# An early-fusion image and text block on one core: projection and FFN as three float32r products each, with low parts by GpSimd, and other steps moved

## What is computed

```
red = grid.mean(axis=(3, 5))                      # mean of a window
q, kv = ln(red) @ la_wq, ln(win) @ la_wkv
local_out = red + softmax(q k) v @ la_proj_w + la_proj_b   # over the 9 cells
patch_out = local_out @ mod_w + mod_b
cls_out = cls + attention(cls, local_out) @ ga_proj_w + ga_proj_b
```

## Time and profile before

| what | value |
|---|---|
| median of 3 runs | 766.26 us (765.4 to 767.36) |
| the profiled execution's own time | 761.81 us |
| its span, first to last instruction | 760.1 us |
| PE busy | 690.5 us, 91% of the span |
| DVE busy | 535.0 us, 70% |
| POOL busy | 422.3 us, 56% |
| ACT busy | 394.8 us, 52% |
| mean granted TensorE clock | 0.960 of 2.4 GHz |
| read and written in HBM | 33.69 MB and 11.40 MB |

### The profile page before, as it was taken

The page is one execution under the profiler, slowest core; times in us unless marked ns, Lnnn a source line. Parts: engine busy times, 40 slices in busy tenths (PEclk is TensorE's granted clock), DMA queues, the critical chain, the costliest instruction groups (busy, mean ns, idle before and its releaser), DMA issues.

```text
span 760.1 us, 23650 instructions
## 1 busy us (share of the span) xinstructions
PE 690.5 (91%) x9239; PEld 550.9 (72%) x9239; DVE 535.0 (70%) x1208; ACT 394.8 (52%) x969; POOL 422.3 (56%) x450
## 2 busy tenths in 40 slices
PE   5998969989987288999999999999999999999873
PEld 3987847778874166778778877878887887887651
DVE  2468585686877457678878878878878878866632
ACT  4563432634542145666666666666566566565431
POOL 3667371483643755475575575575675675663221
PEclk9999988999998589999999999999999999999997
DMA  9950470532220022222332332232232232122100
GB/s 221 237 143 1 119 222 1 145 77 47 62 60 22 19 58 69 76 64 67 79 74 74 77 80 72 77 78 74 74 77 76 73 77 78 39 61 57 35 20 25
DMA packets 69524, 58.69 MB, mean 77 GB/s; under 512 B 30607, under 2 KB 68646, under 8 KB 69286
## 3 DMA queue, kind: packets, MB, share of 16 engines
q1 hardware_dynamic: 69414, 57.18, 29.3%
HBM read 33.69 MB, written 11.40 MB: 59 GB/s over the span
## 4 chain that ended last, share of the span: by engine, by line
PE 75%; DVE 12%; DMA 4%; issue 3%; ACT 3%; POOL 2%; SPq 1%; POOLq 0%; DVEq 0%; ACTq 0%
PE p_a L1309 13%; PE p_c L1309 13%; PE p_s L1369 6%; PE p_conv L764 6%; PE p_o L1381 6%; PE p_kv L764 6%; PE p_n L1389 4%; PE p_c L1429 4%; PE p_s L1351 4%; PE p_a L1335 3%; PE p_s L1365 2%; PE p_mm L764 2%; PE p_c L1410 2%; DMA h<-h_tokens 2%; PE p_n L1395 2%
## 5 line engine op out<-in xcount | busy, mean ns | idle before, releaser
L1244 DVE TENSOR_REDUCE mx<-p_s 87x16 bf16<-87x1392 f32 x64 | 101.6, 1587 | 23.5 <-PE p_s L1351 23.4
L1104 POOL TENSOR_TENSOR t<-t,ss_rs 116x512 f32<-116x512 f32 x48 | 50.9, 1060 | 118.3 <-ACT ss_rs L1151 117.1
L1175 ACT ACTIVATE prT<-p_s 87x1392 f32<-87x1392 f32 x64 | 85.1, 1329 | 58.9 <-PE p_s L1369 57.4
L426 POOL TENSOR_TENSOR xs_lo<-xcols,xs_hi 120x585 fp32r<-120x585 f32 (+1 forms) x45 | 60.5, 1351 | 56.9 <-ACT xs_hi L489 56.9
L1100 POOL TENSOR_TENSOR t<-t 116x512 f32<-116x512 f32 x48 | 61.1, 1274 | 22.9 <-DVE t L1235 22.9
L1369 PE MATMUL p_s<-qr,kr 32*87 32x87 f32 x2048 | 68.4, 256 | 0.0
L1107 POOL TENSOR_TENSOR t<-t,tabs 116x512 f32<-116x512 f32 x48 | 63.0, 1312 | 3.8
L1309 PE MATMUL p_c<-w_f,yT 128*116 128x296 f32 x192 | 58.2, 426 | 2.0 <-ACT yT L1194 0.9
L1369 PEld LDWEIGHTS p_s<-qr,kr 32*87 32x87 f32 x2048 | 60.0, 153 | 0.0
L1365 PE MATMUL p_s<-mxT,pick_row 32*87 32x87 bf16 x1024 | 55.6, 207 | 1.4 <-ACT mxT L1169 1.4
L1381 PE MATMUL p_o<-prT,vp 87*32 87x87 f32 x2048 | 54.7, 246 | 0.0
(11 more groups left out here) (248 smaller groups left out, 1892.5 us busy)
## 6 DMA issues: line engine op xcount, KB each, us to landing
xcols<-in_x_cols SPq DMA_DIRECT2D x12, 822.7 KB, 12.1
h<-h_tokens SPq DMA_DIRECT2D x16, 348.0 KB
out<-out_sb SPq DMA_DIRECT2D x48, 116.0 KB
h_tokens<-in_txt SPq DMA_DIRECT2D x4, 1232.0 KB, 11.7
x<-in_txt_cols SPq DMA_DIRECT2D x32, 154.0 KB, 2.7
qr<-qkT SPq DMA_DIRECT2D x64, 58.0 KB, 2.0
kr<-qkT SPq DMA_DIRECT2D x64, 58.0 KB, 2.0
vp<-vt SPq DMA_DIRECT2D x32, 87.0 KB
```

Of the source, the lines that this page charges most:

```text
L426: nc.gpsimd.tensor_tensor(xs.lo[:, n % XS_SLOTS, :, 0:M].bitcast(F32R), raw, xs.hi[:, n % XS_SLOTS, :, 0:M], ALU.subtract).then_inc(S['xs_ ...
L1104: link(nc.gpsimd.tensor_tensor(t4, t4, ss_rs[:, b].unsqueeze(2).broadcast_to([TP, 2 * HEADS, HD]), ALU.mult))
L1175: nc.scalar.activation(prT[:, k % 2], p_s[0:SEQ, :, 0:QUADS * SEQ], ACT.Exp, scale=HD ** -0.5).then_inc(S['s_exp'], 1)
L1244: nc.vector.reduce_max(mx[:, k % 2, :, 0:QUADS], p_s[0:SEQ, :, 0:QUADS * SP].rearrange("p j (a k) -> p j a k", k=SP)[:, :, :, 0:SEQ], AX_X ...
```

## The change

The projection and the FFN become split products. Their weights get a high part (ScalarE) and a low part (GpSimd) once, in group 0. Their inputs are evicted twice by ScalarE, as they are and rounded to float32r, and GpSimd subtracts one from the other (`oB_lo`, `yT_lo`); TensorE waits for the low part. Beside it: the loads x.1 and x.2 get earlier due times; the centring goes to other cells of windows 2 and 3; the clears are made in two parts, one behind `xc` of group 1, one behind `add.0` of group 0; in the last window the sum over the cells is made by TensorE; the gate's exponential takes the negated maximum as its bias; the last group uses banks A and C in turn; hb of group 0 and the first exponential wait for aggT, not agg. All five tables of the groups are new, with a period of 276 and a start of 2070.

```diff
@@ order tables @@
-                score.2.498 s_max.0.517 att.0.538 sum.0.593 sum.1.638 lo.0.695 lo_var.0.700 patch.0.730 gv.0.752
+                score.2.498 s_max.0.517 att.0.538 sum.0.620 sum.1.638 lo.0.695 lo_var.0.700 patch.0.730 gv.0.752
-WINDOW_SP = table("""x.0.-398 x.1.-64 x.2.-30 rows.0.736 cls.0.970""")
+WINDOW_SP = table("""x.0.-398 x.1.-317 x.2.-245 rows.0.736 cls.0.970""")
...
+                oT.1.510 mT.3.525 oT.2.536 exp.3.542 oB.0.575 oB.1.633 oT.3.647 oB.2.662 oB.3.734 yT.0.762
+                yT.1.778 rstd_c.0.875 ffn.0.881 ffn.1.904 yT.2.916 ffn.2.944 gate.0.1004 twT.0.1086""")
...
+                oN.3.674 oB.3.715 proj.0.722 proj.1.739 yT.0.756 yT.1.771 proj.2.838 ffn.0.869 ffn.1.890
+                yT.2.911 ffn.2.932 twT.0.1072 lora.0.1092 lora.1.1232""")
...
+GROUP_POOL = table("""xc.0.-264 xlo.0.-86 add.0.33 scale.0.63 shift.0.110 add.1.153 scale.1.166 shift.1.177 add.2.220 scale.2.249
+                shift.2.260 hb.0.571 oB_lo.0.599 hb.1.676 oB_lo.1.683 oB_lo.2.688 oB_lo.3.768 hb.2.786
+                yT_lo.0.856 yT_lo.1.880 yT_lo.2.925 base.0.931 above.0.969 base.1.1036 base.2.1070""")
+GROUP_SP = table("""cols.0.-400 rows.0.-276 place.0.210 values.0.258 place.1.291 values.1.438 store.0.1111 store.1.1115 store.2.1253""")
-GROUP_PERIOD, GROUP_START = 288, 2100
+GROUP_PERIOD, GROUP_START = 276, 2070
@@ patch_tokens @@
-        CENTRE_PE, CENTRE_DVE = (3, 5, 6), (3, 4, 6)
-        CLASS_PE, CLASS_DVE = ((1, 2), (1, 4), (1, 6)), ((0, 6), (1, 0), (1, 4), (1, 6))
+        CENTRE_PE, CENTRE_DVE = ((2, 6), (2, 7), (3, 6)), ((2, 5), (2, 6), (3, 5))
+        CLASS_PE, CLASS_DVE = ((1, 2), (1, 4), (1, 6)), ((0, 6), (1, 0), (1, 4), (1, 5))
...
-                    if s == STEPS - 1 and k == 0:
-                        pool.wait_ge(S['conv'], CELLS * STEPS)
-                        pool.wait_ge(S['kv_mm'], CELLS * STEPS)
-                        pool.wait_ge(S['stat'], CELLS * STEPS)
-                        pool.wait_ge(S['red'], (CELLS - 1) * STEPS)
-                        clear()
...
-                if name == 'sum':
+                if name == 'sum' and s < STEPS - 1:
...
-                    pe_.wait_ge(S['agg'], s + 1)
-                    transpose(p_T, agg[0:M], M).then_inc(S['aggT'], 1)
+                    if s < STEPS - 1:
+                        pe_.wait_ge(S['agg'], s + 1)
+                        transpose(p_T, agg[0:M], M).then_inc(S['aggT'], 1)
+                    else:
+                        pe_.wait_ge(S['vw'], PIECES * (s + 1))
+                        for c in range(CC):
+                            part = slice(C + P * c, C + P * (c + 1))
+                            mm_ = mm(p_T[:, c, 0:M], [kv[0:M, ring(s, j), i, part] for j in range(PIECES) for i in range(LOAD_CELLS)]
+                                     + [bias_kv[0:1, part]], [ident[0:M, 0:M]] * CELLS + [consts.ones[0:1, 0:M]])
+                        mm_.then_inc(S['aggT'], 1)
@@ attention_ffn @@
+        LAST_BANK = {'tile': 'ACA', 'gate': 'A', 'lora': 'CA'}
+
+        def bank(what, g, k):
+
+            return LAST_BANK[what][k] if g == GROUPS - 1 else 'C'
...
-            def clear():
-
+            def clear_strips():
+
+                pool.wait_ge(W['conv'], CONVS)
                 for part in (qr, kr, mx):
                     ready(nc.gpsimd.memset(part[:], 0.0))
+
+            def clear_values():
+
+                pool.wait_ge(W['kv_mm'], CONVS)
+                pool.wait_ge(W['stat'], CONVS)
+                pool.wait_ge(W['red'], (CELLS - 1) * STEPS)
                 ready(nc.gpsimd.memset(vp[:, :, :, HD:], 1.0))
                 ready(nc.gpsimd.memset(twT[TILES * LR:TILES * LR + 1], 1.0))
...
+                    if g == 1:
+                        clear_strips()
...
+                    if g == 0 and k == 0:
+                        clear_values()
...
+                if name == 'oB_lo':
+                    pool.wait_ge(S['oB_out'], GB * g + k + 1)
+                    if k == 0:
+                        wait(pool, S['proj'], 3 * (g - 1))
+                    part = (slice(None), half, slice(None), slice(SEQ * k, SEQ * (k + 1)))
+                    nc.gpsimd.tensor_tensor(onT.lo[part].bitcast(F32R), on_raw[:, k % 2], onT.hi[part],
+                                            ALU.subtract).then_inc(S['oB_low'], 1)
+                if name == 'yT_lo':
+                    pool.wait_ge(S['yT_out'], 3 * g + k + 1)
+                    wait(pool, S['ffn'], 3 * g + k - 1)
+                    nc.gpsimd.tensor_tensor(yT.lo[:, b].bitcast(F32R), y_raw[:, b], yT.hi[:, b], ALU.subtract).then_inc(S['yT_low'], 1)
...
+                    if g == 0 and k == 1:
+                        for n, (w, raw) in enumerate(((wp, w_p), (wf, w_f))):
+                            pool.wait_ge(S['w2_high'], n + 1)
+                            nc.gpsimd.tensor_tensor(w.lo[:].bitcast(F32R), raw[:], w.hi[:], ALU.subtract).then_inc(S['w2_low'], 1)
...
+                    if g == 0:
+                        act.wait_ge(W['agg'], STEPS - 1)
+                        act.wait_ge(W['kv_mm'], CONVS)
+                        act.wait_ge(consts.w_in, 16 * consts.LOADS)
+                        act.wait_ge(consts.S['w_sub'], 3 * CC)
+                        nc.scalar.copy(wp.hi[:].bitcast(F32R), w_p[:]).then_inc(S['w2_high'], 1)
+                        nc.scalar.copy(wf.hi[:].bitcast(F32R), w_f[:]).then_inc(S['w2_high'], 1)
...
-                    nc.scalar.copy(onT[:, half, :, SEQ * k:SEQ * (k + 1)],
+                    wait(act, S['oB_low'], n4 - 2)
+                    nc.scalar.copy(on_raw[:, k % 2], p_n[:, 0:CC * SP].rearrange("p (c q) -> p c q", c=CC)[:, :, 0:SEQ])
+                    nc.scalar.copy(onT.hi[:, half, :, SEQ * k:SEQ * (k + 1)].bitcast(F32R),
...
-                    nc.scalar.copy(yT[:, b], p_c[:, 0:CC * TP].rearrange("p (c n) -> p c n", c=CC)).then_inc(S['yT_out'], 1)
+                    wait(act, S['yT_low'], n3 - 2)
+                    nc.scalar.copy(y_raw[:, b], product('tile', g, k)[:, 0:CC * TP].rearrange("p (c n) -> p c n", c=CC))
+                    nc.scalar.copy(yT.hi[:, b].bitcast(F32R), product('tile', g, k)[:, 0:CC * TP].rearrange("p (c n) -> p c n", c=CC)).then_inc(S['yT_out'], 1)
...
-                    nc.scalar.activation(g_e[:], g_e[:], ACT.Exp).then_inc(S['g_exp'], 1)
+                    act.wait_ge(S['ffn_out'], 3 * g + 3)
+                    wait(act, S['tw_ok'], g)
+                    for tile in range(TILES):
+                        last = nc.scalar.activation(g_e[:, tile], f[:, half, tile, C + LR:FFN_N], ACT.Exp, bias=g_max[:, tile:tile + 1])
+                    last.then_inc(S['g_exp'], 1)
...
-                    link(nc.vector.reduce_max(g_max[:], lg, AX_X))
-                    nc.vector.tensor_tensor(g_e[:], lg, g_max[:].unsqueeze(2).broadcast_to([TP, TILES, EXPERTS]),
-                                            ALU.subtract).then_inc(S['g_m'], 1)
+                    wait(dve, S['g_exp'], g)
+                    nc.vector.reduce_max(g_max[:], lg, AX_X, negate=True).then_inc(S['g_m'], 1)
...
-                    mm(p_c[0:TP, 0:C], [onT[:, half, c, TP * k:TP * (k + 1)] for c in range(CC)],
-                       [w_p[:, c] for c in range(CC)]).then_inc(S['proj'], 1)
+                        pe.wait_ge(S['w2_low'], 2)
+                    pe.wait_ge(S['oB_low'], GB * g + min(k + 1, GB - 1) + 1)
+                    mm_split(product('tile', g, k)[0:TP, 0:C], onT.chunks(lambda x_, c: x_[:, half, c, TP * k:TP * (k + 1)]),
+                             wp.chunks(lambda x_, c: x_[:, c])).then_inc(S['proj'], 1)
...
-                    pe.wait_ge(S['yT_out'], n3)
-                    mm(p_c[0:TP, 0:FFN_N], [yT[:, b, c] for c in range(CC)], [w_f[:, c] for c in range(CC)]
-                       ).then_inc(S['ffn'], 1)
+                    pe.wait_ge(S['yT_low'], n3)
+                    mm_split(product('tile', g, k)[0:TP, 0:FFN_N], yT.chunks(lambda x_, c: x_[:, b, c]), wf.chunks(lambda x_, c: x_[:, c])
+                             ).then_inc(S['ffn'], 1)
```

85 lines of the change are left out of this document (39 added, 46 removed).

## The result

| | before | changed |
|---|---|---|
| median | 765.83 us (4 runs, 764.44 to 767.36) | 811.97 us (4 runs, 802.94 to 818.05) |
| ratio | | 1.0563, 95% interval 1.0474 to 1.0651 |
| profiled execution, span | 761.8, 760.1 us | 818.05, 816.3 us |
| PE busy | 91% | 87% |
| ACT, POOL, DVE busy | 52%, 56%, 70% | 53%, 59%, 66% |

The forecast was 735.5 us.

What follows compares the result with a forecast made beforehand. TensorE's own time was taken to bound the steady stage. Products -17.3, weights +1, windows -9, transition -4, banks -3, last chain +1.5 sum to -30.8: 761.8 to 731.0, plus 4.5 for the median, 735.5 us; range 727 to 747.

Steps and rivals of the forecast that it cites:

- The other cover of group 0 (later token loads): Transition: group 0's later token loads have 7 us from due time to first use; no cost was added.
- All five rivals: Queues 0.20, windows give nothing back 0.17, yT low parts never hidden 0.04, products no faster 0.02, all better 0.07.
- the slower one: Steady groups: TensorE idles before each ffn for copy and subtraction, period 30.7, 784 us; chance 0.04.
- The stage table: Groups 3 to 15: TensorE has work in 344.49 of 344.5 us, so only TensorE's own time counts there.
- Products: Projection and FFN tiles: three products save 0.36 us a tile, 1.08 us a group, -17.3 us in all.
- What pays for it: Low parts and second evictions: nothing in the steady stage; weights' low parts in group 0 cost +1 us.
- The rival of the queues: Steady groups: more GpSimd work makes waits more frequent, period 28.2, +9 us, 744.5 us; chance 0.20.
- Windows: Windows 2 and 3: earlier loads and moved centring remove waits and low clock; -9 us, between -3 and -12.
- Transition: Between windows and steady groups: clears moved out of window 4's weightings; -4 us, between -8 and +2.
- The sum: Window 4: 40 records on TensorE, 5.3 us or twice that at low clock, replace 5.8 us of VectorE's sum.
- End: Tail: two banks in turn give -3 us, the last chain's copies and low parts cost +1.5 us.
- the latency's 1.5 us: Tail: a copy and a low part at oB.3 and yT.2 in the last chain, +1.5 us after overlap.

Runs made afterwards that it cites:

- e2: Changed kernel with SyncE's token load due at -310 instead of -276, ahead of the transposed values' transfers; 755.3 us, ratio 0.985.
- e11: Kernel before with only the token load due at -475 instead of -500, behind the transposed values' transfers; 794.81 us, ratio 1.036.
- e18: Changed kernel, all due times kept, with each group's token load issued as two transfers (rows 0 to 111, 112 to 115); 754.95 us, ratio 0.988.
- e3: Changed kernel with float32 projection and FFN, no low parts, single evictions, new order tables kept; 823.92 us.
- e16: e2 with the last window's sum put back on VectorE; 745.26 us.
- e12: e4 with the last window's sum put back on VectorE; 741.38 us, ratio 0.965.
- e9: e2 with the float32 products of before; 758.18 us.
- e10: Whole change on the group order of before, low parts put in behind their evictions; 756.28 us.
- e4: Changed kernel with float32 products and the old group tables, period and start; 748.06 us, ratio 0.976.
- e15: e12 with the FFN product alone in three products, projection still float32; 748.66 us.
- e7: e4 with the windows' input loads back at their old due times on SyncE; 757.84 us.
- e8: e4 with the centring of the weights back at its old cells of window 2; 760.96 us.
- e17: e16 with float32 products from single evictions in the last group only; 744.88 us.

## Why the prediction was wrong

**The step that failed** is the one that cost the later token loads at nothing: "The other cover of group 0 (later token loads) has 7 us from its due time to its first use." Three things were wrong in it. It asked for group 0 alone, where the load comes in every group. It took a distance of due times (7.4 us) for time at hand, and neither looked up how long the load takes to land (8.7 and 8.9 us where its reader waited in the kernel before, 10.1 us at its new place) nor what it stands behind on SyncE; what a moved load stands behind was asked for the windows' loads and not for this one. And it named no one who waits: behind the statistics on VectorE stands `max.1`, and behind that TensorE. e2, e11 and e18 show it, from three sides: issue it earlier, issue it later in the kernel before, make it land sooner. All five rivals and their chances missed it; the slower one (low parts of yT never hidden) had a period of 30.7 us by another mechanism, which e3 refutes.

**The stage table** was read rightly, that the steady stage is TensorE's alone. But a full TensorE says only that nothing was late then, not by how much nothing was late. The load had mostly 9.7 to 10.6 us from issue to first use, and may have needed some 8.8: a margin of one or two microseconds, where the change took away 2.9 by the due times and made the landing longer by more than one.

**Products**, -1.08 us a group: mis-sized. Measured -0.68, -0.03 and +0.86 by the order, and -0.52 between e16 and e12, two kernels without waits for tokens. The tiles themselves gave 0.95 and 0.80 us. The pace of a pair was right (0.28 and 0.24 us), the tile was taken as six of them: first and last pair take 0.05 to 0.09 us more each where a 32-row product follows, and an FFN tile in the changed order takes 0.98 us, not 0.82. The float32 tile depends on its neighbours too: in e9 an FFN tile takes 1.12 to 1.16 us, in e12 0.99 to 1.09.

**What pays for it**, nothing in the steady stage: not so. The low parts are as long as estimated, and TensorE doesn't wait for them by name. But with three products it idles more (0.43 us a group in e10 against e4, 0.41 in e15 against e12, 0.14 in e2 against e9), and products beside them take longer. The rival of the queues had the size (e2's period of 28.43 us is near its 28.2) and in part the kind; its waits for onT_lo and yT_lo are not the ones seen, which are for kr, for h and for ScalarE's eviction.

**Windows**, -9 us: measured -15.1 at group 0's start, past the far end of -12. Both parts are right in kind. The loads were mis-sized: undoing them costs 6.0 us (e7), where they had a share of 2.5, because they take waits out of windows 3 and 4 too. The centring gave 7.3 us (e8) for a net 6.5.

**Transition**, -4 us: measured +4.0. The wait of 12.1 us is 5.6 us in the changed kernel, as forecast. The larger part of the miss is the same late load, which groups 2 and 3 wait for already: with the load issued earlier (e2) the transition is 91.6 us, 1.5 shorter than before, and the late load alone lengthens it from 93.1 to 104.0 us in the kernel before (e11). The sum, weighed as even (5.3 against 5.8 us), is a smaller part: it took its 5.15 us in the changed kernel, but 9.5 us at a granted clock of 0.50 in e4, the prediction's own "twice that". Without it the transition is 90.4 us in the changed order (e16) and 88.0 in the order of before (e12), 2.7 and 5.1 us shorter than before's.

**End**, -1.5 us: measured +7.6. The bank's 3 us fit the means and aren't shown; the latency's 1.5 us are not in the last group (e17). A longer end by the changed order with float32 products, and one more by three products in the groups before the last, were no terms at all.

## What to carry to other kernels

Ahead of moving a load, take three numbers from the trace: when it is issued and behind what, when it lands, and when its first reader starts. A reader without a wait doesn't say how much slack it has; look for a place where the reader of the same load did wait, and read the landing there. The landing changes with the place in the queue. A due time that moves by 2.5 us cost 28 here (e11). Look for a circle (queue, landing, in-order reader, the engine that bounds, and back to the queue): its length becomes the period, whatever the engines' busy shares are. A cheaper product has to be priced from start to start with its neighbours, not from the pace inside a run, and its saving has to be looked for again in the period: here up to all of it went into idle time and slower neighbours.
